# Reordering the first steps and the score maxima of a fused cross-attention and mixture-of-experts block

## The reference

```python
x = x + tanh(g_xattn) * attn(layernorm(x), ctx)      # 8 heads of 64
x = x + tanh(g_ffn) * moe(layernorm(x))              # 8 experts + 1 shared
# attn: keys and values of 512 context and 256 own tokens (768 in all),
#   softmax(q k^T / 8) v, then Wo, bo
# moe: top 2 of 8 gates, gelu(x w1 + b1) w2 + b2, hidden 512; shared expert added to it
```

## Time and profile before

| what | value |
|---|---|
| median of 3 runs | 160.68 us (160.15, 160.68, 160.74) |
| the profiled execution's own time | 159.81 us |
| its span | 157.9 us |
| granted TensorE clock | 1.00 |
| instructions | 4330 |

### The profile page before, as it was taken

One profiled execution on the slowest core, in us unless ns is written; L12 is line 12 of the kernel. 1 busy time (PEld: TensorE's weight loads), 2 busy tenths in 40 slices (PEclk: granted clock), 3 DMA queues, 4 the chain that ended last, 5 costly groups with the idle time before them and its releaser, 6 DMA issues.

```text
span 157.9 us, 4330 instructions
## 1 busy us (share of the span) xinstructions
PE 149.4 (95%) x1775; PEld 114.6 (73%) x1775; DVE 99.5 (63%) x209; ACT 113.7 (72%) x188; POOL 109.8 (70%) x97
## 2 busy tenths in 40 slices
PE   7899889999999999999989789999999999999992
PEld 4646444466665656657768678999999999989992
DVE  2575787777677676876873183535653589896731
ACT  3266787997877968778758989755358688968730
POOL 5459999866955566855599778977199069688740
PEclk9999999999999999999999999999999999999999
DMA  4969992000000000000000000040000000100001
GB/s 128 350 191 289 334 336 61 0 4 0 4 2 8 0 4 0 0 4 0 4 0 4 0 4 0 4 133 0 0 4 0 0 8 0 33 4 0 0 4 33
DMA packets 10269, 7.71 MB, mean 49 GB/s; under 512 B 1117, under 2 KB 8458, under 8 KB 10250
## 3 DMA queue, kind: packets, MB, share of 16 engines
q1 hardware_dynamic: 10250, 7.44, 15.5%
HBM read 7.18 MB, written 0.26 MB: 47 GB/s over the span
## 4 chain that ended last, share of the span: by engine, by line
PE 81%; DVE 6%; ACT 6%; DMA 2%; issue 2%; POOL 1%; SPq 0%; DVEq 0%; ACTq 0%
PE banks L1283 11%; PE banks L995 6%; PE banks L996 6%; PE banks L997 6%; PE banks L1035 5%; PE banks L1051 5%; PE banks L1246 4%; PE banks L1174 4%; PE banks L1176 3%; PE banks L1122 3%; PE banks L1175 3%; PE banks L1090 2%; PE banks L1194 2%; PE banks L1038 2%; DVE part L827 2%; DMA wf<-in_ctx_dram 2%
## 5 line engine op out<-in xcount | busy, mean ns | idle before, releaser
L584 POOL TENSOR_TENSOR p_lo<-prob,p_hi 128x1024 f16<-128x1024 f32 x23 | 49.0, 2128 | 19.4 <-ACT p_hi L678 19.2
L735 ACT ACTIVATE prob<-banks,b1T 128x256 f32<-128x256 f32 x72 | 28.3, 474 | 12.9 <-PE banks L997 9.3
L670 ACT ACTIVATE prob<-banks 128x1024 f32<-128x1024 f32 x24 | 24.5, 1022 | 9.8 <-PE banks L1140 9.8
L827 DVE TENSOR_REDUCE part<-banks 128x2 f32<-128x1024 f32 (+1 forms) x24 | 29.1, 1216 | 1.6 <-PE banks L1095 1.5
L678 ACT ACTIVATE p_hi<-prob 128x1024 f16<-128x1024 f32 x24 | 25.4, 1057 | 0.8
L601 POOL TENSOR_TENSOR k_both<-prob,k_both 128x1024 f16<-128x1024 f32 x8 | 17.5, 2189 | 4.2 <-ACT k_both L743 3.1
L1283 PE MATMUL banks<-ring,prob 128*128 128x128 f32 x160 | 19.6, 276 | 0.0
L1174 PEld LDWEIGHTS banks<-v_hi,p_hi 128*128 128x128 f16 x192 | 17.4, 98 | 2.9 <-issue 2.5
L1174 PE MATMUL banks<-v_hi,p_hi 128*128 128x65 f16 x192 | 19.2, 195 | 0.0
L1175 PE MATMUL banks<-v_lo,p_hi 128*128 128x64 f16 x192 | 19.1, 193 | 0.0
L1176 PE MATMUL banks<-v_hi,p_lo 128*128 128x65 f16 x192 | 19.1, 194 | 0.0
(11 more groups left out here) (138 smaller groups left out, 334.2 us busy)
## 6 DMA issues: line engine op xcount, KB each, us to landing
ring<-in_L_ffn_w_dram SPq DMA_DIRECT2D x16, 256.0 KB, 5.6
wf<-in_ctx_dram SPq DMA_DIRECT2D x2, 256.0 KB, 4.6
wa<-in_L_xattn_Wk_dram SPq DMA_DIRECT2D x2, 256.0 KB, 3.6
wa<-in_L_xattn_Wv_dram SPq DMA_DIRECT2D x2, 256.0 KB, 5.2
ring<-in_L_ffn_ws_dram SPq DMA_DIRECT2D x2, 256.0 KB, 4.9
x_sb<-in_x_dram SPq DMA_DIRECT2D x2, 128.0 KB, 2.8
wa<-in_L_xattn_Wq_dram SPq DMA_DIRECT2D x1, 256.0 KB, 4.6
wa<-in_L_xattn_Wo_dram SPq DMA_DIRECT2D x1, 256.0 KB, 6.3
```

The costliest lines, as they stand in the source:

```text
L584: nc.gpsimd.tensor_tensor(p_lo[:, u % RINGP, :, :].rearrange("p a n -> p (a n)"), prob[:, u % RINGE, :], p_hi[:, u % RINGP, :, :].rearrang ...
L670: nc.scalar.activation(prob[:, u % RINGE, :], units(u).rearrange("p a n -> p (a n)"), ACT.Exp, scale=DH ** -0.5 / S_SCORE).then_inc(exp_do ...
L735: nc.scalar.activation(hid[:, k % NHID, c * T1:(c + 1) * T1], span(2 * (k % 2), HC * T1)[:, c * T1:(c + 1) * T1], ACT.Gelu, bias=b1T[:, e ...
L827: nc.vector.tensor_reduce(dst, src, AX_X, ALU.max).then_inc(part_done, 1)
```

## The change

In the ramp, the item `("k", 0, 1)` goes from step -3 to step -2, so that the third chunk (0, 2) comes ahead of it on PE; the twelve warming matmuls and the wait ahead of them are gone; and chunk (1, 0) leaves step -1 on PE for step 0, behind the scores of unit 0. In every step from 0 on, PE runs `max_chunk` directly behind the scores (ahead of `values` and `shift_row`), and DVE takes its maximum directly behind the low halves of the items (ahead of the tail, `shift_out`, `reciprocals` and `normalise`). The split of the second weights of slot 8, which no product reads, is dropped.

```diff
-W2_STEP = {2: FFN0 + 2, 3: FFN0 + 3, 4: FFN0 + 6, 5: FFN0 + 7, 6: FFN0 + 8, 7: FFN0 + 9, 8: FFN0 + 10}
+W2_STEP = {2: FFN0 + 2, 3: FFN0 + 3, 4: FFN0 + 6, 5: FFN0 + 7, 6: FFN0 + 8, 7: FFN0 + 9}
...
 LATE = {
-    -3: [(("v", 0, 0), 7), (("k", 0, 1), 4)],
-    -2: [(("q", 1), 7)],
+    -3: [(("v", 0, 0), 7)],
+    -2: [(("k", 0, 1), 4), (("q", 1), 7)],
...
@@ scalar
-                if i == -2:
-                    raw_item(("k", 0, 1))
+                    if ITEMS[n] == ("q", 1):
+                        raw_item(("k", 0, 1))
...
@@ vector
+            def chunk_maximum(p, c):
+
+                part_max(p, c)
+                if c == UPP - 1:
+                    whole_max(p)
...
                 if i >= 0:
                     for n in items_at(i):
                         item_of(n)
+                if i >= 0 and chunk_of(i) is not None:
+                    chunk_maximum(*chunk_of(i))
                 for b, s in tail_of(i - 1):
                     tail(b, s)
...
                     normalise(values_of(i))
-                if chunk_of(i) is not None:
-                    p, c = chunk_of(i)
-                    part_max(p, c)
-                    if c == UPP - 1:
-                        whole_max(p)
+                if i < 0 and chunk_of(i) is not None:
+                    chunk_maximum(*chunk_of(i))
...
@@ tensor
                 if 0 <= i < NU:
                     scores(i)
+                if i == 0:
+                    max_chunk(*chunk_of(-1))
+                if i != -1 and chunk_of(i) is not None:
+                    max_chunk(*chunk_of(i))
...
                     shift_row(shift_of(i))
-                if chunk_of(i) is not None:
-                    max_chunk(*chunk_of(i))
                 for n in late_items(i):
                     item_of(n)
-                if i == -2:
-                    pe.wait_ge(part_done, 2)
-                    keep_warm(WARM_STEP, 2)
```

More of the change, by code:

```diff
@@ L136 @@
 NI = len(ITEMS)
-WARM_START, WARM_LAYERNORM, WARM_KEYS, WARM_STEP = 14, 9, 5, 12
+WARM_START, WARM_LAYERNORM, WARM_KEYS = 14, 9, 5
 HI_BY_DVE = [("q0", 0)]
```

## The result

| | before | changed |
|---|---|---|
| median of 19 runs each | 160.42 us | 158.44 us |
| ratio, 95% interval | 1 | 0.988 (0.986 to 0.991) |
| the profiled execution's own time | 159.81 us | 159.00 us |
| its span | 157.9 us | 157.1 us |
| granted TensorE clock in it | 1.00 | 1.00 |

A forecast was written before the change was run, and what follows sets the result against it. PE, busy 95% of the span, was taken as the bound, through the ramp and steps 5 to 19. Terms -0.22 - 1.38 + 1.17 + 0.62 = +0.19 us gave median 160.9, range 159.7 to 162.0.

The forecast's parts named there:

- The ramp: Before step 1's scores: `shift_row(0)` starts 1.10 us earlier, mostly given back to serial reductions; -0.22 us.
- The two waits that go: Steps 7 and 19: PE no longer waits for DVE's reduction before chunk (p, 2); 0.69 us each, -1.38 us.
- The waits that come: Steps 5, 8, 11 and 14: PE waits before chunk (p, 0) for ACT's eviction of keys; +1.17 us.
- Step 17: DVE's maximum of (7, 0) delays the copy that frees bank 7, so PE writes it later; +0.62 us.
- the new waits do not bite: Rival: ACT's eviction or DVE's copy is sooner, only the gains are left; -1.60 us, 159.1, chance 0.15.
- The fall of the clock: Rival: PE's clock drops for the stretch from 16.8 to 21.1 us; +3.9 us, 164.8, chance 0.04.
- the failed ramp: Rival: `shift_row(0)` starts no sooner than about 14.85; +0.88 in place of -0.22, 162.0 in all, chance 0.10.
- the remaining waits: Rival: maxima of (3, 1) and (7, 1) stay late, waits of steps 7 and 19 remain; +1.57, 162.3, chance 0.04.
- The dropped split: One DVE instruction of 2.04 us and one on ACT removed, under a PE that never waits there; nothing.

The follow-up runs named there:

- ramp_only: Changed kernel's ramp kept, with PE's chunk and DVE's maximum in the order of before in all steps from 1 on; 159.84 us, ratio to before 0.997.
- tail_first: Changed kernel with DVE's tail reads put ahead of the chunk's maximum again; 157.35 us, ratio to before 0.982.
- pe_order_only: Changed kernel with PE's order kept and DVE's maximum put back behind `normalise`; 161.89 us, ratio to before 1.011.
- zero128x2: Changed kernel plus two matmuls of zeros of 128 rows between scores and chunk in each of nine steps; 160.03 us, ratio to before 0.999.
- zero64: Changed kernel plus one matmul of zeros of 64 rows between scores and chunk in each of nine steps; 158.35 us, ratio to before 0.988.

## Why the prediction was wrong, by its own steps

- **The ramp (-0.22): right.** -0.28 within the trace, -0.5 (0.2 to 0.8) in the runs of `ramp_only`. `shift_row(0)` came early (14.77, which is 13.66 without the late start of 1.11 us; forecast 13.75), its gain was given back to two serial reductions, and PE idled 1.32 us where 1.3 had been forecast.
- **The two waits that go (-1.38): right**, -0.69 in each of steps 7 and 19.
- **The waits that come (+1.17): right as waits**, 1.23 us by the starts; wrong as lengths of steps (+0.03 in all), since each of these steps also lost two changes of shape.
- **Step 17 (+0.62): right**, 0.62. The copy sets the length of this step; PE's two changes of shape less only made its wait longer, as `tail_first` showed.
- **The failed step.** The sum has a term for each wait that goes or comes, and none for the move of the chunk past `values` and `shift_row`: "the kernel's end moves by what PE wins or loses in the ramp and in steps 5 to 19" was worked out from waits alone, and PE's own work was taken as the same in any order. It is not: a 64-row group between 128-row groups costs 0.22 to 0.31 us more than next to its like, in step 2 too, which the sum left out. That term was missing: -2.11 us over eight steps, and it turned +0.19 into -1.92 (measured within the trace: -1.98). It could have been had from the trace of before: a chunk follows a score group by 0.22 us, a projection follows a chunk by 0.32 (57.73 to 58.05 in step 12 above), a chunk follows the last of `values` by 0.12 (57.61 to 57.73) where two of `values` are 0.03 apart, and `values` follow a score group by 0.31: the row behind the 52.55 of the earlier trace rows, PE of the kernel before, is

```profile
52.86 0.20 PE L1174 MATMUL banks<-v_hi,p_hi 128*128 128x65 f16 x1
```

- **The rivals.** The faster one (the new waits do not bite) gave 159.1 and was nearest in time, for a reason that did not happen: the waits were there. Its 159.1 lies 0.7 us from the 158.44, and that is luck. The fall of the clock (+3.9), the failed ramp and the remaining waits did not occur.
- **The dropped split (0): consistent**, from the scores of unit 23 to the end of the span are 69.1 us before and 69.2 after the change (157.9 - 88.82 and 157.1 - 87.95); it wasn't tried alone.

The expectation for `pe_order_only` was wrong by 2.8 us for another reason: PE asks earlier for banks that DVE frees as late as before, so that steps 6, 7, 9, 12, 15, 18 and 19 became longer than in the changed kernel.

## What to carry to other kernels

Cost an order on TensorE by its neighbours, too: read the start-to-start distance of each kind of pair of groups from the trace (here a chunk starts 0.22 us behind a score group of the same row count, and `values` 0.31) and count the pairs in both orders. Put matmuls of the same row count next to each other, and move the work on the consuming engine in the same edit, or the wait eats the gain. Where a difference comes again and again in steps that share nothing but their order, compare step lengths before looking for waits: no wait list shows this cost.

## What the runs showed of the hardware

- A change from 64-row to 128-row matmuls and back costs 0.20 us in `zero128x2` (0.48 against 0.22 us from score group to chunk, less twice the 0.03 of a matmul), and 0.22 to 0.31 a pair in the steps of the kernel. Whether the array drains or the next weights cannot be loaded ahead, the rows do not separate; that is left open.
- There is a third reading, open as well: 64-row matmuls run two at a time here. A group of four with 256 columns each takes 0.22 us from start to start, 0.055 each, while twelve of 128 rows and 256 columns take 1.31 (13.54 to 14.85), 0.11 each, and the zero matmul of 64 rows in `zero64` starts with the chunk. A matmul of 128 rows does not run beside them in any row here, so a part of the 0.20 us may be that this side-by-side running stops and starts again at the two edges.
- The price is absorbed wherever PE waits anyway: four of nine inserted pairs cost nothing in the end, and in step 17 of the change a wait for DVE hid the saving until `tail_first` took the wait away.
- An idle stretch of 1.32 us on PE, in a kernel busy 94% of the time, left PE at the higher of its two clock levels (granted clock 1.00; a projection of 0.96 us behind it, 0.97 ahead of it), and ten matmuls filling it changed nothing (158.28 against 158.44 us).
- The granted clock of the page does not show every slow stretch. Over the first 4 us of the kernel before it reads 1.00, while the fourteen warming matmuls of the earlier trace rows take 0.23 us each, against 0.11 later on; only the length of a known matmul tells:

```profile
0.00:4.00 4.00, 2.96 (x14) 1.96 (x14) 1.07 (x6) 1.28 (x1) 2.30 (x12) 1.00 0.45 131
```
